# A third pattern slot with a cast shared by two engines, one Exp per chunk, and three int8 slots

## The reference

```python
x = x + attn(layernorm(x)); x = x + ffn(layernorm(x))      # x: 8192 tokens x 2048
# attn, H=16 heads, D=128, M=1024 stored patterns per head
q = (rms_norm(x) @ W_in.T).reshape(B, S, H, D) @ W_q.T
k = stored_patterns @ W_k.T;  v = stored_patterns @ W_v.T   # 16 x 1024 x 128 each
probs = softmax(einsum('bshd,hmd->bhsm', q * sigmoid(beta), k))
retrieved = rms_norm(einsum('bhsm,hmd->bshd', probs, v).reshape(B, S, H*D))
return retrieved + x
# ffn, int8 weights, 2048 -> 8192 -> 2048
return ((silu(x @ w_gate * s_gate) * (x @ w_up * s_up)) @ w_down) * s_down
```

## Time and profile before

| quantity | value |
|---|---|
| median of 3 runs | 2113.75 us (2113.28 to 2114.41) |
| profiled execution, slowest core | 2107.54 us |
| its span (core 2, slowest) | 2105.9 us; the 8 cores 2096.5 to 2105.9 |
| PE, ACT, DVE, POOL busy | 1787.5, 641.0, 212.6, 176.2 us |
| mean granted clock of TensorE, by core | 0.904 to 0.909 of full speed |

### The profile page before, as it was taken

One profiled execution on the slowest core, in us unless ns is written; L12 is line 12 of the kernel. 1 busy time (PEld: TensorE's weight loads), 2 busy tenths in 40 slices (PEclk: granted clock), 3 DMA queues, 4 the chain that ended last, 5 costly groups with the idle time before them and its releaser, 6 DMA issues.

```text
span 2105.9 us, 21035 instructions; the slowest of 8 cores (2096.5 to 2105.9 us)
## 1 busy us (share of the span) xinstructions
PE 1787.5 (85%) x8488; PEld 838.2 (40%) x8488; DVE 212.6 (10%) x447; ACT 641.0 (30%) x732; POOL 176.2 (8%) x239
## 2 busy tenths in 40 slices
PE   3479778888711899999999999999997979899795
PEld 2434334444301344444444444444443434344342
DVE  3300000000077000000000000000000020100202
ACT  4741366666665111111111111111114212222120
POOL 3200110000022000000000000000000010100101
PEclk8679868888855899999999999999998989999898
DMA  9600220000142222221222212222113131221302
GB/s 287 197 1 0 90 91 1 1 1 1 40 177 103 80 80 80 81 78 63 80 80 80 80 64 77 80 80 80 67 54 113 38 105 40 82 63 39 107 16 60
DMA packets 42373, 154.70 MB, mean 73 GB/s; under 512 B 6181, under 2 KB 6182, under 8 KB 36902
## 3 DMA queue, kind: packets, MB, share of 16 engines
q0 software_dynamic: 23984, 84.00, 11.9%
q1 hardware_dynamic: 18294, 69.35, 10.1%
HBM read 103.10 MB, written 16.78 MB: 57 GB/s over the span
## 4 chain that ended last, share of the span: by engine, by line
PE 79%; ACT 7%; DMA 5%; DVE 4%; issue 3%; POOL 1%; SPq 0%; DVEq 0%; ACTq 0%; POOLq 0%
PE PS L968 21%; PE PS L983 20%; PE PS L1108 19%; PE PS L484 5%; PE PS L579 3%; PE PS L610 3%; PE PS L594 2%; DMA out<-arena 2%; DMA arena<-patT 2%; PE PS L643 1%; ACT arena L619 1%; ACT arena L332 1%; ACT arena L404 1%; ACT arena L461 1%; ACT srow_s L630 1%
## 5 line engine op out<-in xcount | busy, mean ns | idle before, releaser
L1108 PE MATMUL PS<-arena 128*128 128x512 bf16 x1956 | 451.0, 385 | 45.7 <-DVE arena L1047 36.0
L968 PE MATMUL PS<-arena 128*128 128x512 bf16 x2048 | 455.0, 380 | 5.6 <-DMA arena<-wu 5.6
L983 PE MATMUL PS<-arena 128*128 128x512 bf16 x1984 | 438.7, 379 | 0.0
L1108 PEld LDWEIGHTS PS<-arena 128*128 128x128 bf16 x1956 | 193.3, 99 | 288.3 <-issue 65.0
L968 PEld LDWEIGHTS PS<-arena 128*128 128x128 bf16 x2048 | 201.1, 98 | 248.8 <-issue 9.0
L992 ACT ACTIVATE arena<-PS,sgc_s 128x1024 bf16<-128x1024 f32 x64 | 71.3, 1114 | 735.5 <-PE PS L977 735.5
L983 PEld LDWEIGHTS PS<-arena 128*128 128x128 bf16 x1984 | 194.0, 98 | 234.2
L1075 ACT ACTIVATE arena<-arena 128x2048 bf16<-128x2048 int8 x64 | 121.7, 1908 | 341.7 <-PE PS L1097 332.1
L619 ACT ACTIVATE arena<-PS 128x512 bf16<-128x512 f32 x256 | 137.1, 598 | 39.5 <-PE PS L610 39.5
L1000 DVE TENSOR_TENSOR arena<-arena 128x1024 bf16<-128x1024 bf16 x64 | 44.3, 693 | 851.4 <-ACT arena L995 851.4
L484 PE MATMUL PS<-arena 128*128 128x512 bf16 x496 | 117.2, 390 | 8.2 <-ACT arena L461 8.2
(11 more groups left out here) (108 smaller groups left out, 921.9 us busy)
## 6 DMA issues: line engine op xcount, KB each, us to landing
arena<-wg POOLq DMA_DIRECT2D x64, 512.0 KB, 3.5
arena<-wu POOLq DMA_DIRECT2D x64, 512.0 KB, 4.2
arena<-win SPq DMA_DIRECT2D x16, 1024.0 KB, 7.4
arena<-x SPq DMA_DIRECT2D x16, 1024.0 KB, 7.8
arena<-wd SPq DMA_DIRECT2D x64, 256.0 KB, 2.6
arena<-patT SPq DMA_DIRECT2D x16, 512.0 KB, 4.6
x1sp<-arena SPq DMA_DIRECT2D x8, 1024.0 KB, 4.3
arena<-x1sp POOLq DMA_DIRECT2D x32, 256.0 KB, 4.8
```

The costliest lines, as they stand in the source:

```text
L968: En.matmul(PG[:, half * 512:half * 512 + 512], wgb[:, hc * 128:(hc + 1) * 128], x1nT3[:, hc, half * 512:half * 512 + 512], start=(hc == 0 ...
L983: En.matmul(PU2[:, half * 512:half * 512 + 512], wub[:, hc * 128:(hc + 1) * 128], x1nT3[:, hc, half * 512:half * 512 + 512], start=(hc == ...
L1108: En.matmul(PS[:, j * 512:(j + 1) * 512], fuse3[:, ic, j * 128:(j + 1) * 128], wdb[:, c * 512:(c + 1) * 512], start=(ic == 0), stop=(ic == ...
```

## The change

It has three parts. In stage E the f32 patterns get a third slot, and the cast of each head is divided: POOL takes columns 0 to 639, ACT columns 640 to 1023; PE waits for both, and a load waits for both casts of head h-3. In stage F the two Exps of a chunk become one of 1024 columns, behind both score matmuls, and scores wait for the whole Exp of chunk K-2. In stage I the int8 weights have three slots, and a load waits for the convert of group gi-3. (An unused region, `ksq`, gives its place to the third slot.)

```diff
-        O_PATF = [reg("patf0", 73728, 4096, 3, 3), reg("patf1", 77824, 4096, 3, 3)]
-        O_KSQ = [reg("ksq0", 69632, 2048, 3, 3), reg("ksq1", 71680, 2048, 3, 3)]
+        O_PATF = [reg("patf0", 73728, 4096, 3, 3), reg("patf1", 77824, 4096, 3, 3),
+                  reg("patf2", 69632, 4096, 3, 3)]
...
-            if h >= 2:
-                wait(Ry, cG, pat_cv[h - 2])
-            dma(Ry, sW[h % 2], patf, patT_d[h])
-            ldv = sW[h % 2].n
-            wait(Rg, sW[h % 2], ldv)
+            if h >= 3:
+                wait(Ry, cG, pat_cv[h - 3])
+                wait(Ry, cS, pat_cv2[h - 3])
+            dma(Ry, sW[h % 3], patf, patT_d[h])
+            ldv = sW[h % 3].n
+            wait(Rg, sW[h % 3], ldv)
             if h >= 2:
                 wait(Rg, cT, e_mm_val[h - 2])
             tcv = cG.tick()
             Rg(lambda En, pat=pat, patf=patf:
-               En.tensor_copy(pat, patf).then_inc(cG.h, 1))
+               En.tensor_copy(pat[:, 0:640], patf[:, 0:640]).then_inc(cG.h, 1))
             pat_cv[h] = tcv
+            wait(Rs, sW[h % 3], ldv)
+            if h >= 2:
+                wait(Rs, cT, e_mm_val[h - 2])
+            tcv2 = cS.tick()
+            Rs(lambda En, pat=pat, patf=patf:
+               En.activation(pat[:, 640:1024], patf[:, 640:1024],
+                             AF.Copy).then_inc(cS.h, 1))
+            pat_cv2[h] = tcv2
             wait(Rt, cG, tcv)
+            wait(Rt, cS, tcv2)
...
-                for half in range(2):
-                    if K >= 2:
-                        wait(Rt, cS, exp_halves[K - 2][half])
-                    t1h[half] = cT.tick()
-                    Rt(... scores of this half ... .then_inc(cT.h, 1))
-                for half in range(2):
-                    wait(Rs, cT, t1h[half])
-                    Rs(... En.activation(eT half, psb half, AF.Exp).then_inc(cS.h, 1))
+                if K >= 2:
+                    wait(Rt, cS, exp_vals[K - 2])
+                for half in range(2):
+                    Rt(... scores of this half; the second one counts cT, t1 ...)
+                wait(Rs, cT, t1)
+                t2 = cS.tick()
+                Rs(lambda En, mc=mc, psb=psb:
+                   En.activation(eT[:, mc * 1024:(mc + 1) * 1024], psb, AF.Exp).then_inc(cS.h, 1))
...
-            i8s = gi % 4
+            i8s = gi % 3
-            if gi >= 4:
-                wait(Ry, cS, wd_cv[gi - 4])
+            if gi >= 3:
+                wait(Ry, cS, wd_cv[gi - 3])
```

More of the change, by code:

```diff
@@ L152, in _build_nc @@
         O_WD = [reg("wd%d" % i, i * 4096, 4096, 7, 7) for i in range(6)]
-        O_WD8 = [reg("wd8_%d" % i, 24576 + i * 2048, 2048, 7, 7) for i in range(4)]
+        O_WD8 = [reg("wd8_%d" % i, 24576 + i * 2048, 2048, 7, 7) for i in range(3)]
         O_SDREP = reg("sdrep", 163840, 8192, 7, 7)
@@ L163, in _build_nc @@
         for name in ["sA0", "sA1", "sA2", "sB0", "sB1", "sB2", "sB3", "sC0", "sC1",
-                     "sW0", "sW1", "sW2", "sW3", "dX0", "dX1", "dSo0", "dSo1",
+                     "sW0", "sW1", "sW2", "dX0", "dX1", "dSo0", "dSo1",
                      "sXr0", "sXr1", "sXr2", "sXr3",
@@ L168, in _build_nc @@
         sA = [sems["sA0"], sems["sA1"], sems["sA2"]]
-        sW = [sems["sW0"], sems["sW1"], sems["sW2"], sems["sW3"]]
+        sW = [sems["sW0"], sems["sW1"], sems["sW2"]]
         sB = [sems["sB0"], sems["sB1"], sems["sB2"], sems["sB3"]]
@@ L502, in _build_nc @@
         pat_cv = [None] * H
+        pat_cv2 = [None] * H
         for h in range(H):
             pat = bfv(O_PAT[h % 2], 1024)
-            patf = f32v(O_PATF[h % 2], 1024)
+            patf = f32v(O_PATF[h % 3], 1024)
             PK = PS[:, (h % 2) * 1024:(h % 2) * 1024 + 1024]
             PV = PS[:, 2048 + (h % 2) * 1024:2048 + (h % 2) * 1024 + 1024]
-            if h >= 2:
-                wait(Ry, cG, pat_cv[h - 2])
-            dma(Ry, sW[h % 2], patf, patT_d[h])
-            ldv = sW[h % 2].n
-            wait(Rg, sW[h % 2], ldv)
+            if h >= 3:
[4 more added lines that the diff above has]
+            wait(Rg, sW[h % 3], ldv)
             if h >= 2:
@@ L564, in _build_nc @@
         exp_vals = []
-        exp_halves = []
         uevac_val = [None] * H
@@ L603, in _build_nc @@
                 psb = PS[:, p * 1024:p * 1024 + 1024]
-                t1h = [None, None]
+                if K >= 2:
+                    wait(Rt, cS, exp_vals[K - 2])
                 for half in range(2):
-                    if K >= 2:
-                        wait(Rt, cS, exp_halves[K - 2][half])
-                    t1h[half] = cT.tick()
[L609 to L613, removed]
@@ L614, in _build_nc @@
-                eh = [None, None]
-                for half in range(2):
-                    wait(Rs, cT, t1h[half])
[L617 to L623, removed]
@@ L624, in _build_nc @@
-                exp_vals.append(eh[1])
+                    if half == 1:
+                        t1 = cT.tick()
+                        Rt(lambda En, psb=psb, h=h, mc=mc, half=half:
+                           En.matmul(psb[:, half * 512:half * 512 + 512],
+                                     kT[:, h * 1024 + mc * 128:h * 1024 + (mc + 1) * 128],
+                                     qT[:, h * 1024 + half * 512:h * 1024 + half * 512 + 512],
+                                     start=True, stop=True).then_inc(cT.h, 1))
+                    else:
+                        Rt(lambda En, psb=psb, h=h, mc=mc, half=half:
+                           En.matmul(psb[:, half * 512:half * 512 + 512],
+                                     kT[:, h * 1024 + mc * 128:h * 1024 + (mc + 1) * 128],
+                                     qT[:, h * 1024 + half * 512:h * 1024 + half * 512 + 512],
+                                     start=True, stop=True))
@@ L625, in _build_nc @@
+                wait(Rs, cT, t1)
+                t2 = cS.tick()
+                Rs(lambda En, mc=mc, psb=psb:
+                   En.activation(eT[:, mc * 1024:(mc + 1) * 1024], psb, AF.Exp).then_inc(cS.h, 1))
+                exp_vals.append(t2)
                 if mc >= 1:
```

## The result

The changed kernel takes 2142.30 us in the median of 9 runs, the kernel before 2114.08 in 10; the ratio is 1.0126, with a 95% interval from 1.0109 to 1.0144. It is 26.6 us slower. The forecast was 14.7 us slower, 2128.5 us, with a range up to 2137: the sign was right, the size was not, and the measured time lies outside the range. (In some executions the cores of a die run at a lower granted clock and take longer; the ratios leave these out, the medians don't.)

The account below looks back on a forecast made before the run. It took stage E as bound by pattern loads and the POOL cast, stage F by PE's loop with hardly anything to spare. The median 2113.75 plus 9.5 (E), 5.2 (F) and 0 (I) gave 2128.5 us, range 2118 to 2137.

Parts of the forecast that it names:

- The circle: Stage E: each head runs serially through ACT cast, PE k matmuls, ACT k and v evacuations, then the next cast; +9.5 us.
- I take 3.52: Stage E: time per head in us, chosen between 3.60 at the low clock and 3.17 at the full one.
- ACT end to PE start 0.15: Stage E: gap in us from the end of ACT's cast to PE's start, read from stage F's rows.
- the stalls: Stage F: PE waits 0.14 us for the larger Exp in every second chunk, 0.385 us per head at the full clock.
- 5 heads in 6: Stage F: share of heads counted as paying the stalls, low-clock iterations costing nothing; this gave +5.2 us.
- Rival C: Stage F: PE's new loop gaps cost one more low-clock chunk per head, 21 us on top, 2149 us; chance 0.05.
- The top of the range for this stage: Stage F: an Exp of 1.19 us makes the shortage 0.31 us and the stage +13 us.
- Stage I: Three int8 slots instead of four: loads land within the cover of the converts, so the change in time is 0.

Follow-up runs that it names:

- e_ahead: Stage E's part of the change alone, with each head's casts written one head earlier; ratio 0.9951 to the kernel before, stage E 42.6 us.
- e_wfirst: Stage E's part alone, with PE's long-fulfilled wait for head h-2's k evacuation written ahead of the cast waits; ratio 1.0055 to the kernel before, E 62.5 us.
- f_tail: The kernel before, plus an idle 384-column ACT copy at the start of each head's serial tail; ratio 1.0094, stage F 301.2 us.
- f_pad: Stage F's part of the change alone, plus 192 columns of idle ACT copy in each head's tail; ratio 1.0043 to the kernel before, F 291.0 us.

## Why the prediction was half right

**Stage E, the mechanism: right.** The circle, its members and their order stand in the trace as worked out, the loads dropped out, and e_ahead opens the circle for -21.4 us.

**Stage E, the size: +12.8 us on average against +9.5, just outside its bound of +12.** The step "I take 3.52" failed, and with it "ACT end to PE start 0.15". The turn is 3.71 us. Of the difference 0.09 us is the wait that stands behind the blocking one, shown by e_wfirst. I took the gap from stage F; the earlier trace rows give 0.15 too (242.91 to 243.06), but for the first head, which lacks that wait. The third head, with it, had the longer gap already, 0.26 us from POOL's end at 248.68 to PE's start at 248.94:

```profile
247.64 1.04 POOL L517 CAST arena<-arena 128x1024 bf16<-128x1024 f32 x1 [3.14 <-DMA arena<-patT]
```

0.08 us is the clock, 0.52 instead of the 0.59 carried over. Before, the full clock came mostly for a head behind two that stood 1.7 us apart, as at 248.94; in the circle heads stand 3.7 us apart, and the clock was the low one from the first cast to the end of the stage on every core. 0.03 is the cast, 0.53 instead of 0.50. Fifteen turns of 0.19 are 2.9 us. The rest is small: the first cast starts 4.7 us into the stage on average, before 4.5 (on core 1, 5.7).

**Stage F, the stalls: right.** 0.14 us in every second chunk, Exp of 1.02 us, 0.35 us per shortest head against 0.385 forecast.

**Stage F, the size: +14.2 us against +5.2.** This is the larger miss. The sentence that failed is the count "5 heads in 6", with the low-clock chunks taken as a fixed number. Their number depends on how long a head is, and 0.35 us more made it 92 long heads of 120 instead of 54, 8.6 us in all. f_tail shows that such a loss needs no gap, and f_pad that it mostly goes when the same loop is padded. Rival C had the clock falling, at 0.05, for the wrong reason: the loop's gaps. Its price was 21 us; the clock's share was under half of it. The top of the range for this stage, given as +13 (by its own terms 14), meets the measured size by luck: it stood for an Exp of 1.19 us, and the Exp took 1.02.

**Stage I: right**, no change within what can be told, 0.28% either way.

**The sum.** The two stages as measured make 12.8+14.2 = 27.0 us, and the ratio gives 26.6. This leaves out the +4.0 us of stage I in that execution, so the agreement is in part luck; the share of the slowest core and of stage I's own variation isn't settled by these runs.

The Trainium skill, "Perfetto Trace Analysis", Optimizing Scalar/DVE Operations, had the sign of stage F: ACT was busy 176.41 of 299 us and the larger Exp did not relieve it but left a bubble of 0.14 us on PE in every second chunk. In stage E, too, what ACT does mattered less than when, as e_ahead shows.

## What to carry to other kernels

Before work is given to an engine with time to spare, write down what stands ahead of and behind it there in program order: with the same cast in one place or the other the stage took 64.0 or 42.6 us. Try the plain cure, more slots, alone first: the third slot without the split gave all of the gain (41.8 us), and a fourth 4.8 us more. And where a serial tail returns at a fixed interval and the clock falls in it, a few tenths of a microsecond more or less per turn are worth more or less than their length: time a lengthened tail beside the change, or what the clock gains or loses is taken for the change's own doing.

## What the hardware showed that I had not expected

A longer tail can make the stage shorter: 0.4 us more per head cost 15.8 us in stage F, 0.6 us more cost 4.4. A wait that has long been fulfilled costs 0.10 us if it stands behind one that blocks (0.24 against 0.14 us from ACT's end to PE's start). ACT evacuations that follow each other without a break report growing durations, 1.02 to 1.14 us, at an even spacing of 0.90.
